# Four of eight blocks of x turned by VectorE in quarters of 32 tokens, with GpSimd merging the quarters' moments

## The reference

```python
x = L0_attn_x                                    # (2, 2048, 1024), float32
x = x + attn(_layernorm(x), Wqkv, bqkv, Wo, bo)  # one head, d = 256: qkv, softmax(q k / 16) v, times Wo
x = x + ffn(_layernorm(x), ...)                  # relu(h up)^2 down, plus a gated low-rank path, layernorm, gamma, beta
def _layernorm(x, eps=1e-5): return (x - mean) / sqrt(var + eps)
```

## Time and profile before

| | us |
|---|---|
| median of 3 runs (2320.28 to 2321.04) | 2320.76 |
| the profiled execution, its own time | 2322.11 |
| its span, first to last instruction | 2320.3 |
| TensorE busy | 2307.1 (99%) |
| VectorE busy | 1578.0 (68%) |
| ScalarE busy | 794.3 (34%) |
| GpSimd busy | 281.0 (12%) |

### The profile page before, as it was taken

One profiled execution on the slowest core, in us unless ns is written; L12 is line 12 of the kernel. 1 busy time (PEld: TensorE's weight loads), 2 busy tenths in 40 slices (PEclk: granted clock), 3 DMA queues, 4 the chain that ended last, 5 costly groups with the idle time before them and its releaser, 6 DMA issues.

```text
span 2320.3 us, 27515 instructions
## 1 busy us (share of the span) xinstructions
PE 2307.1 (99%) x10888; PEld 1939.1 (84%) x10888; DVE 1578.0 (68%) x1772; ACT 794.3 (34%) x885; POOL 281.0 (12%) x550
## 2 busy tenths in 40 slices
PE   9999999999999999999999999999999999999998
PEld 8988988888888878888888888888888888888886
DVE  7787649887989765598763378774249876424548
ACT  4333336666555441522221331213132121223211
POOL 3000000000223200033100023210003220000000
PEclk9999999999999999999999999999999999999999
DMA  8999854532334699978996678898668999666865
GB/s 309 333 359 363 300 193 164 198 122 80 122 120 144 224 314 334 317 276 313 342 308 197 191 275 299 312 335 262 193 219 274 320 331 320 209 193 206 239 209 194
DMA packets 232801, 580.83 MB, mean 250 GB/s; under 512 B 26208, under 2 KB 80096, under 8 KB 232288
## 3 DMA queue, kind: packets, MB, share of 16 engines
q1 hardware_dynamic: 151392, 443.52, 58.1%
q10 hardware_dynamic: 81280, 135.55, 16.0%
HBM read 421.96 MB, written 152.83 MB: 248 GB/s over the span
## 4 chain that ended last, share of the span: by engine, by line
PE 92%; DVE 3%; DMA 1%; SPq 1%; ACT 1%; issue 1%; POOL 1%; ACTq 0%; DVEq 0%; POOLq 0%
PE psum L1116 11%; PE psum L1117 11%; PE psum L1118 11%; PE psum L1095 10%; PE psum L1096 10%; PE psum L1097 10%; PE psum L930 3%; PE psum L928 3%; PE psum L929 3%; PE psum L968 2%; PE psum L998 2%; PE psum L970 2%; PE psum L969 2%; PE psum L1000 2%; PE psum L999 2%; PE psum L948 1%
## 5 line engine op out<-in xcount | busy, mean ns | idle before, releaser
L1751 DVE TENSOR_TENSOR HB<-HB,psum 128x1024 f32<-128x1024 f32 x135 | 163.0, 1217 | 299.1 <-PE psum L1097 299.1
L1972 POOL TENSOR_SCALAR veA<-mvA 128x1 f32<-128x1 f32 x32 | 31.2, 976 | 1269.0 <-DVE mvA L1659 1269.0
L1341 ACT ACTIVATE HB<-HB 128x1024 f32<-128x1024 f32 x64 | 67.8, 1060 | 307.6 <-DVE HB L1751 307.6
L1095 PE MATMUL psum<-XS2h,WR 128*128 128x512 f32 x280 | 109.4, 391 | 1.0 <-DVE XS2l L1457 0.7
L1095 PE MATMUL psum<-XS1h,WR 128*128 128x512 f32 x280 | 109.3, 390 | 0.3 <-DMA WR<-wu_s 0.2
L1095 PE MATMUL psum<-XS0h,WR 128*128 128x512 f32 x280 | 109.1, 390 | 0.0
L1095 PE MATMUL psum<-XS3h,WR 128*128 128x512 f32 x280 | 109.1, 390 | 0.0
L1097 PE MATMUL psum<-XS0h,WR 128*128 128x512 f32 x280 | 109.0, 389 | 0.0
L1096 PE MATMUL psum<-XS1l,WR 128*128 128x512 f32 x280 | 109.0, 389 | 0.0
L1096 PE MATMUL psum<-XS2l,WR 128*128 128x512 f32 x280 | 109.0, 389 | 0.0
L1097 PE MATMUL psum<-XS1h,WR 128*128 128x512 f32 x280 | 109.0, 389 | 0.0
(11 more groups left out here) (402 smaller groups left out, 6616.6 us busy)
## 6 DMA issues: line engine op xcount, KB each, us to landing
WR<-wu_s SPq DMA_DIRECT2D x280, 512.0 KB, 4.3
WR<-wd_s SPq DMA_DIRECT2D x280, 512.0 KB, 4.7
att_s<-ATT ACTq DMA_DIRECT2D x32, 516.0 KB, 3.4
RAW<-in_x_dram SPq DMA_DIRECT2D x32, 512.0 KB, 8.2
RES<-x1b_s SPq DMA_DIRECT2D x128, 128.0 KB, 5.6
out_dram<-ZR ACTq DMA_DIRECT2D x118, 128.0 KB, 5.5
xT_s<-XT SPq DMA_DIRECT2D x24, 512.0 KB, 7.5
HB<-xT_s SPq DMA_DIRECT2D x12, 1024.0 KB, 8.8
```

The costliest lines, as they stand in the source:

```text
L1095: e.matmul(o, w[:, 0, ws], h[:, :, ws], start=kt == 0, stop=False)
L1751: e.tensor_tensor(to, a, src, op=ALU.add).then_inc(*vevac.next(key))
```

## The change

Blocks 0 to 3 keep their transposes on TensorE, but share the buffers otherwise: raw x always goes to `RAW[0]`, and `ln_norm` writes the normalized x to `RAW[1]` with its columns regrouped (position k·4 + q for partition group q), so that all blocks see the model dimension in the same permuted order. `Wq`, `Wv` and the router's weights are loaded in that order: `load_qkv` issues 27 transfers where it issued 8.

Blocks 4 to 7 take another way:

- `load_x` loads four column quarters of 256, each into 32 partitions: partition 32·a + r holds columns 256a to 256a + 255 of the 16 tokens 32g + r, in runs of 1 KB.
- `x_stats` (VectorE): 16 BN_STATS of 256, without aggregates. Each partition knows only a quarter of a row's moments.
- `x_merge` (GpSimd): six small instructions, a 16 KB store to DRAM, four loads of it (all four quarters to every partition), thirteen instructions that merge, eight for 1/sqrt and the bias; nine more put mean and deviation where the second half wants them.
- `x_norm` (ScalarE): 16 activations of 256 with scale and bias, in place.
- `x_turn` (VectorE): four STREAM_TRANSPOSE of 128x1024 in 32x32 blocks; they write `XAT`, which lies on the low half of `XA`.
- `x_parts`: high parts on ScalarE, low parts on VectorE, from SBUF.

```diff
+    for u in range(4, 8):
         b = 12 * (u - 1)
+        load, moments, norm, parts = (22, 26, 39, 43) if u == 4 else (b - 17, b - 13, b + 1, b + 5)
         for tt in range(4):
+            at(load, "load_x", u, tt)
+            at(moments + tt, "x_stats", u, tt)
+        at(moments + 3, "x_merge", u)
+        for j in range(4):
+            front(norm + j // 2, "x_norm", u, j)
+            at(norm + 1 + j // 2, "x_turn", u, j)
+            front(parts + j, "x_parts", u, j)
...
-    WQR = at("WQR", [128, 4, 8, 128], F32, 144.5)
+    WQR = at("WQR", [128, 4, 4, 256], F32, 144.5)
...
+        def x_norm(u, j):
+            on.wait_ge(*inv["x", u])
+            for g in range(4 * j, 4 * j + 4):
+                k = e.activation(x_rows(u)[:, g], x_rows(u)[:, g], AF.Identity, bias=NBX[:, g:g + 1], scale=RX[:, g:g + 1])
...
+        def x_stats(u, j):
+            for a in range(4):
+                on.wait_ge(*x_in[u % 2][a][u])
+            if u > 4:
+                on.wait_ge(*inv["off", u - 1])
+            for g in range(4 * j, 4 * j + 4):
+                k = e.bn_stats(STX[:, g, :], x_rows(u)[:, g])
...
+        def x_turn(u, j):
+            on.wait_ge(*v_mm[u - 2, 3])
+            on.wait_ge(*hi["norm", u, j])
+            e.transpose(XAT[u % 2][:, :, 128 * j:128 * j + 128].rearrange("p k (g r) -> p g k r", g=4),
...
+            e.dma_start(stat_s[u % 2], SQ[:, :]).then_inc(*sq_st.next(u, by=16))
+            on.wait_ge(*sq_st[u])
+            for a in range(4):
+                e.dma_start(STA[32 * a:32 * a + 32], stat_s[u % 2].rearrange("(q r) n -> r q n", q=4)).then_inc(
...
         def load_x(t, tt):
+            if 0 < t < 5:
+                on.wait_ge(*normed[t - 1, tt if t == 1 else 3])
+            elif t > 4:
+                on.wait_ge(*raw_done(t - 2))
+            if t > 3:
+                src = x[512 * t:512 * t + 512, 256 * tt:256 * tt + 256].rearrange("(g r) n -> r g n", r=32)
+                e.dma_start(x_rows(t)[32 * tt:32 * tt + 32], src).then_inc(*x_in[t % 2][tt].next(t, by=16))
+                return
```

More of the change, by code:

```diff
@@ L139, in timetable @@
 def timetable():
-    order, later = [], {}
+    order, later, ahead = [], {}, {}
     def do(*step):
@@ L147, in at, with front @@
         later.setdefault(n, []).append(step)
+    def front(n, *step):
+        ahead.setdefault(n, []).append(step)
     def run(n):
-        for step in later.pop(n, ()):
+        for step in ahead.pop(n, []) + later.pop(n, []):
             if callable(step[0]):
@@ L217, in timetable @@
     do("ln_norm", 0, 3)
+    for tt in range(4):
+        do("load_x", 1, tt)
     do("e2_mm", 0, 1)
@@ L262, in timetable @@
         at(5 + a, "xt_lo", 1, a)
[L264 to L268, removed]
+    for u, load, moments, norm, turns in ((2, 4, (9, 9, 9, 9), (11, 11, 12, 12), (13, 14, 15, 16)),
+                                          (3, 13, (17, 17, 18, 18), (20, 20, 21, 21), (25, 27, 29, 31))):
+        for tt in range(4):
+            at(load, "load_x", u, tt)
+            at(moments[tt], "ln_stats", u, tt)
+            at(norm[tt], "ln_norm", u, tt)
+        at(moments[3], "ln_rstd", u, 0, 4)
+        for a, n in enumerate(turns):
+            at(n, "xt_tr", u, a)
+            at(n, "xt_hi", u, a)
+            front(n + 1, "xt_lo", u, a)
+    for u in range(4, 8):
         b = 12 * (u - 1)
+        load, moments, norm, parts = (22, 26, 39, 43) if u == 4 else (b - 17, b - 13, b + 1, b + 5)
         for tt in range(4):
[L271 to L279, removed]
+            at(load, "load_x", u, tt)
+            at(moments + tt, "x_stats", u, tt)
[4 more added lines that the diff above has]
+            front(parts + j, "x_parts", u, j)
     for q, n0, times in ((("d", 1, 0), 68, (70, 71, 72, 72, 72, 73)), (("d", 1, 1), 75, (77, 78, 79, 79, 79, 80)),
@@ L456, in timetable @@
                 run(56 + g)
-    assert not later, list(later)
+    assert not later and not ahead, (list(later), list(ahead))
     def chunk(c):
@@ L663, in transformer_layer @@
     RAW = [at(f"RAW{i}", [128, 4, 1024], F32, 176.5 + 16 * i) for i in range(2)]
+    XAT = [at(f"XA{i}t", [128, 8, 512], F32, 128.5 + 32 * i) for i in range(2)]
     OUT = at("OUT", [128, 3, 512], F32, 208.5)
@@ L802, in xt_bank, with wq_parts, wg_parts, raw_done @@
         return 2 * (a % 2) if u == 0 else 6 - 2 * (a % 2)
+    def wq_parts(i, W):
+        return W[:, i].rearrange("p (k q) n -> p k q n", k=2), WQR[:, i].rearrange("p q (k n) -> p k q n", k=2)
+    def wg_parts(W):
+        return W[:, :, 256:264].rearrange("p (k q) n -> p k q n", k=2), GRP[:, :, :].rearrange("p q (k n) -> p k q n", k=2)
+    def raw_done(u):
+        return normed["turn", u, 3] if u > 3 else xt_mm[u, 3]
+    def x_rows(u):
+        return RAW[u % 2][:, :, :].rearrange("p t (b n) -> p (t b) n", n=256)
     def v_bank(t, tt):
```

172 lines of the change are left out of this document (131 added, 41 removed).

## The result

The changed kernel takes 2342.3 us (median of 6 runs, 2337.3 to 2346.6), the kernel before 2320.9 beside it: ratio 1.009, 95% interval 1.008 to 1.010. It is **slower by 21.4 us**; forecast were 5.3 us less. The profiled execution took 2346.55, its span is 2344.7. The whole difference arises in QKV: attention's first matmul starts at 312.72 us before and at 336.99 after, and what follows it takes 2007.6 and 2007.7 us.

What follows compares the result with a forecast made beforehand. TensorE (busy 2307.1 of 2320.3 us) and, in QKV, full transfers bound the kernel. Of 14.1 us of removed transposes, buffer q0's loop lets 5.3 through, added work costed as hidden: 2320.76 - 5.3 = 2315.5 us, range 2307 to 2328.

Steps and rivals of the forecast that it cites:

- The 14.1 us of transposes: TensorE in QKV: 16 batches of eight transposes at 0.88 us each removed, 14.1 us if it never waits.
- The loop of q0: Quads' buffer q0 (load, split, store, next load): already as fast as it can, 36 us a turn, limiting the gain.
- 257.8 - T: Formula for the whole gain, 14.1 us at most; with T = 252.5 it gave 5.3 us.
- T: Time of ScalarE's first key split, at the end of q0's loop: 253.82 before, 252.5 us forecast after.
- g = 76: TensorE's group in block 6 that needs `qk_out(6, 0)`; forecast to start behind an idle time of some 7 us.
- The turn's price: VectorE: four turns a block at 1.25 us in, four norms of 0.81 out, +1.8 us, covered by slack.
- The time that it had: GpSimd's merge, from last moments to `qk_out(b/12, 0)`: about 30 us for a merge of 27, so costed at nothing.
- the sum of 34: GpSimd's merge: some 34 us instead of 27 if contention with VectorE puts its instructions nearer 0.80 us.
- I take 1 us on each later landing: Loads of x in 1 KB runs into 32 partitions: bounds 0 to +8.2 us each; 1 us added to T.
- the second rival: Nothing left: q0's loop gets no faster or slower, T 254 to 261, 2317 to 2324, say 2320 us; chance 0.26.
- waits of a few us before g = 76 don't count beside it: TensorE in QKV: earlier short waits cost nothing, as the gain was set by T alone.
- Eight activations of 256: ScalarE, ahead of `qk_out(6, 0)`: 0.32 us each, 2.6 us, where a high part of about 1 us stood.

Runs made afterwards that it cites:

- e16: Kernel before, with only VectorE's turn replacing TensorE's transposes for blocks 4 to 7 and the parts read from it: 2321.0 us beside 2321.4.
- e12: Kernel before, with one transpose of each eight left in blocks 4 to 7 and nothing added: 2318.1 us beside 2321.7.
- e6: Changed kernel's front part alone (weight order, x through RAW0 into RAW1, its times), all 256 transposes kept: 2328.2 us beside 2321.6.
- e1: Changed kernel, x of blocks 4 to 7 loaded as before, into 128 partitions in runs of 4 KB: 2333.7 us.
- e13: Changed kernel with one of the four activations in each x_norm: 2335.5 us.
- e17: e6 with other times for block 2's norms and for loads, moments and transposes from block 3 on: 2324.1 us beside 2321.2.
- e2: Changed kernel, each load of x for blocks 4 to 7 into 32 partitions in runs of 4 KB: 2338.7 us.
- e3: Changed kernel, each load of x for blocks 4 to 7 into 128 partitions in runs of 1 KB: 2332.0 us.
- e4: Kernel before, x of blocks 4 to 7 loaded in quarters of 32 partitions, 1 KB runs, moments waiting for all four: 2335.4 us.

## Why the prediction was wrong

**The account.** Against the kernel before: removal and turn -0.4 (e16; -3.5 by e12 and +3.1), front part +6.6 (e6), form of the loads +8.6 (after less e1). That is 14.8 of 21.4; the 6.6 left are what e1 has beyond e16 and e6: moments of 256 that wait for all four loads, x_norm on ScalarE, the merge. e13 (-6.8) hints that it's mostly the activations. Adding them up takes it that the parts don't help or hurt each other, which no run tested, and by the intervals each part is known to some 3 us.

**Right.** The 14.1 us of transposes, by the page's count. The loop of q0 as the reason why little of it would come through: e12's two long stops hang on it, though through VectorE's list and not through `qk_out(6, 0)`. That 257.8 - T with T unmoved is 4.2, and the removal alone gave 3.5, is in part luck: e12's interval is 0.5 to 4.6, and its profile has gained nothing when attention starts. After the change the step does stand where it was forecast: `qk_out(6, 0)` ends at T + 11.9 (T + 10.7 forecast), and g = 76 starts then, behind a stop of 2.56 us (some 7 forecast). With T = 279.16 the formula gives 257.8 - 279.16, 21.4 us slower, as measured; so what failed is T. The exact figure is luck, since TensorE came to that point only 2.56 us early, held by the stops before it.

The turn's price (1.25 forecast, 1.23), moments of 256 by columns (16 take 5.5, eight of 512 took 5.4), and the merge came out too: 27 us forecast, it took 26.5 for block 4 (136.33 to 162.88) and 25.4 to 27.4 for the others. The time that it had, which I put at about 30 us, was 27.5 for block 6: its first instruction starts at 215.22, its bias is there at 242.60, and ScalarE's queue is free for `x_norm` at 242.73. The rule of the Trainium skill (GPSIMD Engine Reference, Key points) that I had weighed for the merge, contention with VectorE, is seen in the trace, though the sum of 34 isn't. The same instruction took 0.22 us in block 4 and 2.17 in block 5, beside an instruction of VectorE with two SBUF inputs, and both ended within 0.1 us of each other:
```profile
162.00 0.22 POOL L2119 TENSOR_TENSOR RX<-RX,TX 128x16 f32<-128x16 f32 x1
...
193.58 2.17 POOL L2119 TENSOR_TENSOR RX<-RX,TX 128x16 f32<-128x16 f32 x1
```
```profile
193.39 2.28 DVE L1697 TENSOR_TENSOR QR0a<-QR0a,QH0a 128x2048 fp32r<-128x2048 f32 x1
```
The start: 0.5 us of delay.

**The step that failed: x's landings, "I take 1 us on each later landing".** By block their medians went from 8.5, 8.5, 8.6 and 10.2 us to 11.9, 13.8, 9.5 and 15.8, so by 0.9 to 5.6, and block 5's last piece, which is the one that `x_stats` waits for, took 18.9 where before it took 10.6. I had written the mechanism down under the second rival ("loads into 32 partitions hold up the stores beside them", "each quarter would then load at half speed"), and then let it only slow q0's loop. I priced a landing as a delay of a buffer; it is a **delay of an engine**. VectorE takes its list in order, so `x_stats` waiting 9.95 us held the quad's low parts, these ScalarE's stores, and these `qk_out`. The question that I put to the merge (who is queued behind the waiting instruction) I never put to `x_stats`, nor did I ask how much time its load had. By e1 this step is worth 8.6 to 9.6 of the 21.4 us; the rest is in the steps below.

**The second: "waits of a few us before g = 76 don't count beside it".** I took T as fixed at 252.5, so that earlier stops were free. But T is itself made of turns in VectorE's and ScalarE's lists; with every stop TensorE, VectorE and the quads slipped together, and T came at 279.16: the sums of quad 8 started at 217.33 (199.63 before), those of quad 10 at 258.46 (230.79).

**Sizes.** Eight activations of 256: 4.04 us, not 2.6; 0.50 for one where 512 take 0.56, so almost nothing scales with columns there. I took 0.32 from bounds of 0.28 to 0.56, near the wrong one. The front part's times, costed at nothing, 3.7 us, and 2.9 more that stay open. And no term at all for the clock, which at full 1.00 in all of before's windows gave no hint of what a stop takes with it: 10.4 us here, beside 25.6 of stops.

**Open.** What the front part's last 2.9 us are (e17's stops are 0.5); why e12 is 2 to 3 us faster though its attention starts at 312.78 against 312.72. What follows attention's start is the same work in every kernel here, and it takes 2005.3 us in e12's profile, 2007.6 in the one before and up to 2008.2 in the others, so a single profile's end is no finer than that. What started the stop of 3.83 us at 211.00, behind which no landing stands. And which of the activations, the moments and the merge makes how much of the 6.6 us, beyond e13's hint.

## What to carry to other kernels

Where two resources are full, taking work from one gives what the other lets through: here 3.5 of 12.3 us (0.5 to 4.6), while 4.5 MB less beside the same change gave 9.4. Before an edit turns a load into a slower form, find the instruction that waits for it, take the time from the load's issue to it, and read what stands behind that one in its engine's list, engine by engine, up to the bound one. And a kernel whose bound engine never waits has everything to lose from new waits: price a stop at its length and, where it brings one, the slow stretch behind it, here 1.6 to 2.9 us each.

## What the runs showed of the hardware

- Loads into 32 partitions ran at 216 GB/s from 184 to 190 us with the DMA share at 1.06, so the share alone looks like a full pipe. The stores beside them landed later as well: those of 1 MB from quads' buffer q0 took 15.1 us in e2 and 11.0 in e1 (medians, issued from 100 to 260). The length of the runs, 1 or 4 KB, made no difference over 128 partitions (2332.0 for e3, 2333.7 for e1).
- After a stop of 8.48 us TensorE's steps of 512 columns took 0.43 us for 4.86 us, 0.228 else. Such stretches followed five of the seven places where it stopped in QKV, and cost 1.6 to 2.9 us each; the stops there were 2.0 (four together) to 8.48 us long, and those of 3.25 and 1.16 us brought none. Around a stop of 10.6 (e4) the 20 us windows show clocks of 0.86 and 0.88.
- A small instruction of GpSimd took 2.17 us beside one of VectorE with two inputs in SBUF, and 0.22 without.
- An activation of 128x256 takes 0.50 us from start to start, one of 128x512 0.56.
